# Causal attention on one NeuronCore: two pairs of heads by turns, scores issued for four heads together

## The reference, cut to what matters

```python
q = split_heads(x @ Wq.T + bq)                       # the same for k and v
q_lr = jnp.einsum('bhtd,hdr->bhtr', q, Wq_lsr)       # 16 channels to 32; k_lr too
scores = jnp.einsum('bhir,bhjr->bhij', q_lr, k_lr) / sqrt(32)
attn = softmax(where(causal, scores, -inf))
y = jnp.einsum('bhij,bhjd->bhid', attn, v)
x = layernorm(x + y @ Wo.T + bo)
```

## Time and profile before

| | |
|---|---|
| median of three runs | 2994.31 us |
| the profiled execution | 3000.08 us, span 2998.5 us |
| mean granted clock of PE over the span | 0.923 |
| busy over the span: PE, DVE, ACT, POOL | 2634.7, 1804.4, 1377.6, 1127.7 us |
| PE's score matmuls of this stage, first to last start | 2152.5 to 2522.6 us |
| a row extremum waits for scores: DVE idle in the loop | 137.4 us |

### The profile page before, as it was taken

One profiled execution on the slowest core, in us unless ns is written; L12 is line 12 of the kernel. 1 busy time (PEld: TensorE's weight loads), 2 busy tenths in 40 slices (PEclk: granted clock), 3 DMA queues, 4 the chain that ended last, 5 costly groups with the idle time before them and its releaser, 6 DMA issues. The chain is left out here.

```text
span 2998.5 us, 46699 instructions
## 1 busy us (share of the span) xinstructions
PE 2634.7 (88%) x18034; PEld 1522.7 (51%) x18034; DVE 1804.4 (60%) x3563; ACT 1377.6 (46%) x2409; POOL 1127.7 (38%) x596
## 2 busy tenths in 40 slices
PE   6999989989977789999977799996899998877698
PEld 2334434434433245454536666775455555665487
DVE  3888998998997477777683022223355555555323
ACT  4566566566553366767562111111455544232142
POOL 2888988988987033333340400004100000200030
PEclk8999999999999889999987899998999978988599
DMA  7032032032020633334333401112200000200020
GB/s 270 1 120 113 8 120 113 8 119 113 8 112 7 199 65 80 90 82 93 66 87 152 176 24 36 32 32 65 69 1 1 1 1 1 92 1 1 17 84 29
DMA packets 130762, 201.75 MB, mean 67 GB/s; under 512 B 8144, under 2 KB 106576, under 8 KB 118384
## 3 DMA queue, kind: packets, MB, share of 16 engines
q1 hardware_dynamic: 127472, 190.37, 19.5%
q0 software_dynamic: 3072, 8.39, 0.9%
HBM read 169.12 MB, written 29.62 MB: 66 GB/s over the span
## 5 line engine op out<-in xcount | busy, mean ns | idle before, releaser
L213 POOL TENSOR_TENSOR m_h<-m_h,m_bc 128x1024 f32<-128x1024 f32 x256 | 612.2, 2411 | 83.8 <-DVE m_h L528 83.8
L528 DVE TENSOR_TENSOR_SCAN m_h<-m_da,m_h 128x1024 f32<-128x1024 f32 x256 | 578.1, 2275 | 39.7 <-ACT m_da L418 39.7
L286 PE MATMUL m_psy<-m_h,m_ident 128*128 128x512 f32 x1024 | 496.7, 617 | 23.1 <-POOL m_h L213 23.1
L418 ACT ACTIVATE m_da<-m_dt,m_a_neg 128x511 f32<-128x511 f32 x512 | 330.7, 680 | 157.7 <-DVE m_h L528 154.4
L921 POOL TENSOR_SCALAR c_pr<-c_pr,c_share 128x512 f32<-128x512 f32 x128 | 200.0, 1562 | 398.0 <-DVE c_share L1206 398.0
L286 PEld LDWEIGHTS m_psy<-m_h,m_ident 128*128 128x128 f32 x1024 | 197.2, 197 | 290.3 <-issue 235.4
L515 DVE TENSOR_TENSOR m_h<-m_dtx,m_bc 128x1024 f32<-128x1024 f32 x192 | 231.8, 1208 | 31.8 <-PE m_psy L286 25.8
L981 PEld LDWEIGHTS c_psO<-c_pT,c_vr 32*64 32x64 f32 x8192 | 130.5, 136 | 133.6 <-issue 130.6
L981 PE MATMUL c_psO<-c_pT,c_vr 32*64 32x128 f32 x8192 | 162.5, 288 | 33.6 <-ACT c_oT L1099 29.2
L232 PE MATMUL m_rot<-m_xT,m_in_w 128*128 128x512 f32 x240 | 127.2, 656 | 69.8 <-ACT m_gz L392 51.0
L1086 ACT ACTIVATE c_pr<-c_pr,c_low 128x512 f32<-128x512 f32 x256 | 180.8, 707 | 2.9 <-DVE c_low L1198 2.7
(11 more groups left out here) (346 smaller groups left out, 4385.8 us busy)
## 6 DMA issues: line engine op xcount, KB each, us to landing
m_bc<-bc_dram SPq DMA_DIRECT2D x32, 2048.0 KB, 7.9
c_vr<-v_dram SPq DMA_DIRECT2D x128, 256.0 KB, 4.5
v_dram<-c_stage SPq DMA_DIRECT2D x32, 256.0 KB, 2.1
e_up<-in_up SPq DMA_DIRECT2D x8, 1024.0 KB
e_down<-in_down SPq DMA_DIRECT2D x8, 1024.0 KB
xs_dram<-m_ys SPq DMA_DIRECT2D x1, 4992.0 KB, 34.2
e_buf<-xs_dram SPq DMA_DIRECT2D x39, 128.0 KB, 2.2
y_dram<-e_buf SPq DMA_DIRECT2D x39, 128.0 KB, 1.7
```

Source lines behind the costliest of these rows:

```text
L213: pool.tensor_tensor(hq, hq, bc[:, 1, NP * s:NP * (s + 1), :], ALU.mult).then_inc(p_ready, 1)
L286: mm = pe.matmul(bank, ident[:], h[:, n % HB, e, :], start=False, stop=(s == NG - 1 and e == NP - 1))
L418: ins = act.activation(da[:, n % 2, e, at:at + L - 1], dt[:, u, j, at:at + L - 1], ACT.Exp, scale=a_neg[:, u, j, NP * s + e:NP * s + e + 1])
L528: dve.tensor_tensor_scan(flat, decay, flat, 0.0, ALU.mult, ALU.add).then_inc(scanned, 1)
```

## The change

Within a group the two pairs now alternate: unit n is block `n % 8 // 2` of the pair `n % 2`, so the units of a group have t = 0, 0, 1, 1, 2, 2, 3, 3. The table of items and the helpers follow from it. And PE issues the scores of two units, n + 2 and n + 3, together in every even step; they are the four heads of the group, at the same t, on the four row groups. The wait stands before the first of the two and asks for all units before n + 2.

```diff
-        PER_PAIR = 6
-        ITEMS = ((0, 1), (1, 2), (2, 4), (4, 6))
+        ITEMS = (0, 1, 2, 3, 4, 6, 8, 10, 12)
...
         def item(n):
-            pair, t = divmod(n, LT)
-            return PER_PAIR * pair + ITEMS[t][0], PER_PAIR * pair + ITEMS[t][1]
+            q, o = divmod(n, 8)
+            return 12 * q + ITEMS[o], 12 * q + ITEMS[o + 1]
+
+        def tile(n):
+            return n % 8 // 2
...
                 def scores(n):
                     b, u = divmod(n, UNITS)
-                    pair, t = divmod(u, LT)
-                    if n >= 2:
-                        pe.wait_ge(s_read, 2 * (n - 1))
+                    t, e = tile(n), (tile(n) + 1) * P
+                    if n % 2 == 0 and n >= 2:
+                        pe.wait_ge(s_read, 2 * n)
                     for i in range(2):
-                        h = 2 * pair + i
-                        at, m, e = RANK * (h % QH), h // QH, (t + 1) * P
+                        h = QH * (u // 8) + 2 * (u % 2) + i
+                        at, m = RANK * (h % QH), h // QH
...
-                    if n + 2 < TOTAL:
+                    if n + 2 < TOTAL and n % 2 == 0:
                         if (n + 2) % UNITS == 0:
                             pe.wait_ge(x_free, numbers[n - 30 + 19, "proj"] + 1)
                         scores(n + 2)
+                        scores(n + 3)
                     if n < TOTAL:
                         turn(n)
```

More of the change, by code:

```diff
@@ L1915, in blocks @@
                 return [(i, k) for i in range(2) for k in range(t + 1)]
-            return [(m - ITEMS[t][0], k) for k in range(t + 1)]
+            return [(m, k) for k in range(t + 1)]
         with nc.Block() as block:
@@ L2002, in turn @@
                             pe.wait_ge((t_dve, t_act)[m % 2], m // 2)
-                        for at, (i, k) in enumerate(blocks(n % LT, m % PER_PAIR)):
+                        for at, (i, k) in enumerate(blocks(tile(n), m - first)):
                             mm = pe.transpose(psT[:, m % 2, at * P:(at + 1) * P], pr[:, n % 3, i, k * P:(k + 1) * P], ident[:])
@@ L2123, in softmax @@
                 def softmax(n):
-                    e = (n % LT + 1) * P
+                    e = (tile(n) + 1) * P
                     for i in range(2):
@@ L2131, in keep_turned @@
                     first, last = item(n)
-                    t, q = n % LT, n // 8
+                    t, q = tile(n), n // 8
                     for m in range(first, last):
@@ L2139, in keep_turned @@
                         if t < 2:
-                            i = n // LT % 2 * 2
+                            i = n % 2 * 2
                             act.copy(pT[:, q % 2, i:i + 2, t:4 * t + 1:3, :],
@@ L2143, in keep_turned @@
                         else:
-                            i = n // LT % 2 * 2 + 1
+                            i = n % 2 * 2 + 1
                             act.copy(pT[:, q % 2, i, t:4 * t + 1:3, :],
@@ L2207, in row_max @@
                 def row_max(n):
-                    t = n % LT
+                    t = tile(n)
                     if n == 0:
```

## The result

| | before | changed |
|---|---|---|
| median (range), 4 runs each | 2997.84 us (2987.41 to 3006.3) | 2957.02 us (2948.52 to 2961.83) |
| profiled execution (span) | 3000.08 us (2998.5) | 2954.84 us (2953.2) |
| loop, first scores to last sums | 380.1 us | 328.0 us |
| of it at clock 0.50 | 82.0 us in 5 stretches | 17.0 us in 5 stretches |
| mean granted clock of the span | 0.923 | 0.929 |

The profiled executions differ by 45.3 us: the loop is 52.1 us shorter and what follows it 1.9, but the first scores start 8.7 us later (2161.2 against 2152.5).

What follows compares the result with a forecast made beforehand. TensorE (PE) bounds the loop. About 16 us gained at full clock less 22 lost to half clock makes it 6 us slower: 3006 on the profiled execution, 3000 on the median; range 2967 to 3030 for 8 in 10.

Steps and rivals of the forecast that it cites:

- The clock: Half-clock stretches in the loop: 10 falls of 16 at 5.5 us, 55 in place of 33, 22 us lost.
- four heads for the price of two: Score matmuls on PE: four heads cost what two cost, 2.96 us less a group, 47 us for 16 groups.
- S4: PE's score step for a pair of heads at t = 3 (512 columns): 1.06 us at full clock.
- chain o=2 / o=4 / o=6 / o=0: Pairs of units by place in the group: each takes 3.95, 5.4, 3.35, 3.1 us, with DVE's chain or PE binding.
- plain group: Group without projections at full clock: 15.8 us against 16.4, 0.6 us gained.
- full clock in all: Loop at full clock: nine projection groups x 1.6, six without x 0.6, less 2: about 16 us gained.
- first rival: Clock falls no more often than now (five times, 27 us): 22 us faster, 2972; chance 0.20.
- third rival: Wait on row maxima doesn't bind, PE stays the bound, 47 us come in but for few falls: 2955; chance 0.05.
- S1: PE's score step for a pair of heads at t = 0 (128 columns): 0.42 us at full clock.
- nearly 4: Speedup assumed for four row tiles of K=32, N=512 in the scores, where the skill gives 3.07.
- The added wait: Scores of n+2 wait for row maxima of n and n+1; plain groups gain 0.6 us of 2.96.
- statistics and normalising: DVE work in the last batch's second group, no projection over it: 2.3 and 1.8 us, of which 2 lost.

Runs made afterwards that it cites:

- e11: Kernel before with each score matmul contracting over 64 rows a head instead of 32 (scores become sums over two heads): 2932.99 us, ratio 0.9911.
- e12: e2 with scores over 64 rows a head instead of 32: 2944.44 us, ratio 0.9946.
- e1: Changed kernel's new order of units alone, with the wait and unit-by-unit score issue of the kernel before: 2976.1 us, ratio 0.9916.
- e2: Changed kernel with the second pair's scores issued behind the first turn, so two heads at a time: 3006.73 us, ratio 1.0026.
- e3: Kernel before, old order, with the new wait and both units' scores issued in the even step: 3010.67 us, ratio 1.0017.
- e8b: Changed kernel with the four heads' scores issued behind the first turn instead of ahead of it: 2968.64 us, ratio 1.0029.
- e6: e4 with the next sequence's projections moved to other units, where PE waits for DVE: 2900.11 us, ratio 0.9794.
- e4: Changed kernel with keeps of turned items shared by unit (DVE odd units, ACT even): ratio 0.9824, loop 322.1 us.
- e5: Changed kernel with score matmuls filling 64 of 128 output partitions, so half of the scores' rows: 2909.65 us, ratio 0.9825.

## Why the prediction was wrong, by its own steps

The loop was to lose 16 us at full clock and to pay 22 more for the clock. It gave 52.1 back. The clock is priced by e11's 33.0 us for 78.6 at half clock, 0.42 a us: before's 82 us are then 34, the changed kernel's 17 are 7. So the clock gave 27 us and the rest, 25, came at full clock. By the 0.26 a us between the changed kernel's own two runs its 17 us cost 4.5, and the split is 30 and 22; I give the first, and it is good to some 3 us.

| step | forecast | measured |
|---|---|---|
| what before's 82 us cost | about 33 us | 34 (e11: 33.0 for 78.6) |
| falls after the change, in the loop | 10 | 5 (3 in the second run) |
| length of a stretch | 13.6 us, 5.5 us lost | 3.4 us, 0.9 to 1.5 lost |
| clock in all | 22 us lost | 27 to 30 gained |
| four heads for the price of two | 1.06 us from S4 to the turn | 1.07 |
| chain o=2 / o=4 / o=6 / o=0 | 3.95 / 5.4 / 3.35 / 3.1 | 3.78 / 5.14 / 3.19 / 3.16 |
| plain group | 15.8 us | 15.27 |
| full clock in all | 16 gained | 22 to 25 gained |

**The step that failed is "The clock".** It went: what follows the sums is now "thinner than any of the five places, and it comes 16 times", so the clock falls ten times and stays low as long as it did. Both halves were wrong: five falls came, of 3.4 us, 17.0 us at half clock in place of 136. I counted PE's waits and the lack of scores, attend parts and projections, and took transposes for thin work. Four of the five falls that are left do begin where I put them, 3.4 to 3.8 us after the start of a group's sums; this is the timeline of PE at 2408.2:

```profile
2406.89 0.63 PE L2033 MATMUL a_psX<-a_ident,a_shareB 128*128 128x128 f32 x4
2408.13 0.75 PE L1991 MATMUL a_psS<-a_qkl 32*128 32x128 f32 x8 [0.61 <-DVE a_low L2218]
2408.81 3.46 PE L2003 MATMUL a_psT<-a_ident,a_pr 128*128 128x128 f32 x16
2412.20 0.71 PE L1991 MATMUL a_psS<-a_qkl 32*128 32x256 f32 x8
```

The fifth, at 2439.0, is not at the sums but 6.7 us ahead of them, in the group of the last batch that has the statistics, and ends a wait:

```profile
2439.09 1.66 PE L1991 MATMUL a_psS<-a_qkl 32*128 32x384 f32 x8 [1.93 <-DVE a_low L2218]
```

Behind a fall like that at 2408.2 come sixteen transposes, each over all 128 rows, and at their end the clock is full again. In the kernel before, transposes alternate with scores over 64 of the 128 rows, and the clock stayed low for 13.6 us or more in four places of five, for 34.1 in one. That the rows matter in the kernel before is shown by e11: instruction for instruction the same program, with only the rows of the scores doubled, loses 78.6 of its 82 us at half clock. e12 shows it a second time.

What keeps the clock up in the changed kernel is a question of its own, and I can't put it down to its four row groups. e1 has the new order alone, with two row groups at work, and is at half clock for 10.2 us, no longer than the changed kernel. So the gain of the clock is there with the order alone. Once the wait is added and the second pair's scores stand behind the first turn (e2), it is mostly gone (54.6 us), and issuing the four heads together brings it back (17.0). Which property of the order does it stays open.

PE's waits don't explain it alone either. e3 and e8b have twelve and fifteen stretches and wait more than the kernels they were made from (PE is idle for 27.7 us of the loop against 11.5, and for 60.8 against 36.6). But e6, idle for 27.2 us, has 10.2 at half clock, where e3 has 99.0. The first rival, "the clock falls no more often than now", named the right count (five), but at 27 us for five stretches of the old length; nobody in my list had them short. The third rival has nearly the measured number, 2955, but not what happened: its condition was that the wait on the row maxima doesn't bind, and it binds. That its number came out is luck.

**The rule of the Trainium skill.** The Trainium skill ("TensorE: Matmul & The Clock Gate", "HAM oscillation — how this bites in real kernels") lays falls to long idle gaps. As the rows show it, that account is not enough here: e11 leaves the waits of the program as they are (PE is idle for 13.5 us of the loop against 11.5) and removes nearly all of the half clock, and e2's stretch of 30.7 us has PE at work for all but its first 0.3 us. The first rival, which I hung on it, had the count right and the price wrong. I did not follow it, and then put a rule in its place (thin work means transposes and waits) that was no better founded.

**Four heads for the price of two** held to 0.01 us at 512 columns, and so did 0.64 and 0.86 at 256 and 384; S1 took 0.56 where 0.42 stood in the sum. All four score forms, in the loop by form (busy us, mean ns of one):

```profile
L1991 PE MATMUL a_psS<-a_qkl 32*128 32x512 f32 x128 | 18.2, 640 | 4.6 <-DVE a_low L2218 4.6
L1991 PE MATMUL a_psS<-a_qkl 32*128 32x384 f32 x128 | 15.6, 557 | 1.9 <-DVE a_low L2218 1.9
L1991 PE MATMUL a_psS<-a_qkl 32*128 32x256 f32 x128 | 11.4, 426 | 1.2 <-DVE a_low L2218 1.2
L1991 PE MATMUL a_psS<-a_qkl 32*128 32x128 f32 x128 | 8.9, 350 | 8.6 <-DVE a_low L2218 7.8 <-issue 0.7
```

They sum to 54.1 us busy; the same 512 matmuls took 116.2 before, in part at the lower clock. The Trainium skill ("TensorE: Matmul & The Clock Gate", "Measured speedup vs the span model") gives 3.07 for four row tiles. The 0.15 us more at S4 that I had estimated from it did not come: eight passes of four heads take 1.14 us, four passes of two heads 1.13. Its ratio itself isn't tested, since no run has one head's scores of 512 columns alone. My "nearly 4" isn't shown either: what is shown is that four heads cost what two cost.

**The added wait** binds as forecast: in the plain group PE waits 1.03 us in o=4 (forecast 1.2, here in two waits, one of them for a keep), 0.57 in o=6 (0.9) and 0.76 at the end of o=2 (1.0). The three steps that DVE's chain sets are 0.16 to 0.26 us shorter than my sums (the sum has inverting at 0.83, and the rows at 2319.42 have keep and inverting together in 1.22 where I had 1.38), so the plain group gains 1.1 us instead of 0.6 (15.27 against 16.4). e4 confirms the chain from the other side: with a keep taken off it, the group falls to 14.2. DVE's wait for scores went down by 38% where I had said a third.

**Full clock, 25 for 16.** The groups with projections gained 1.8 to 2.3 us (28.6 to 26.7, 26.3 to 24.0, e11's 21.9 to 20.1 and 23.4 to 21.2; 28.6 to 28.2 where a fall lies in it) against 1.6, the plain ones 1.0 to 1.1 against 0.6, and the 2 us that statistics and normalising were to take in the last batch weren't lost (18.5 in e11, 16.8 here, with a short fall in it). Those are sizes of terms; the mechanism stands.

The range failed because its bounds for the clock went from 5 to 16 falls of one and the same price. The price was the unknown, and no bound stood on it.

## What to carry to other kernels

When a stretch of matmuls falls to half clock, look at the order of the instructions and at how many of the array's rows they use: either one, changed alone, took most of the half clock out of this loop (e1, e11). Packing small contractions onto all four row groups gave the second pair's passes for nothing; it did not keep the clock up by itself (e8b). Bound not only how often the clock will fall but how long it stays down; where nothing in the trace prices that, the cheapest test is the kernel before with one property changed (here 64 rows for 32). And if one engine takes over as the bound of a step, move work that the other engines can do off its chain (the keeps), and put PE's free work where it waits.

## What the runs showed of the hardware that I had not expected

- The granted clock moved with the rows of the array that the scores use: with 64 rows a head instead of 32, and nothing else changed, the time at 0.50 went from 82.0 to 3.4 us, and from 54.6 to 23.8 in the other kernel. Halving the output partitions (e5) did not bring the falls back, though few scores lay where it would have shown.
- It moved nearly as much with the order of the units alone, at two row groups and with PE busy for 95% of the loop: from 82.0 to 10.2 us (e1). And with four row groups in every scores call it could be at 0.50 for 105.4 us (e8b).
- Half clock cost less than its share: 0.42 us of loop a us in e11 against the kernel before, 0.41 in e12 against e2, 0.26 between the two runs of the changed kernel, whose PE has waits to fill.
- Slow stretches were 3.4 us long in the changed kernel and up to 34.1 in the kernel before. 34.1 us of half clock came about with PE busy for all of it.
- Falls sit at fixed places: those of the kernel before were the same to 0.1 us in two executions of different batches, counted from the loop's first scores; of the changed kernel's, three agreed to 0.2 us and two did not come again.
- The mean clock over the span is no measure of this: 0.923 against 0.929, for a loop that went from 0.89 to 0.97.
- What stays open: why the order alone (e1) keeps the clock up with two row groups, why the changed kernel's stretches are short, and how rows, order and waits weigh against each other. No run here separates them.
